# Reads of a DRAM trip moved from the sync engine's queue to ScalarE's, x loaded in 512 B rows, slot numbers read ahead of a wait

## The reference

```
w, sel = top_k(softmax(router_logits), 2); w = w / w.sum(-1)          # per batch
mlp(x, g, u, d) = (gelu(x @ g) * (x @ u)) @ d                         # 256 -> 1024 -> 256
x = x + sum_e dense_w[b, e] * mlp(x, skill_e) + mlp(x, shared)        # layer 0, 8 experts
x = x + x @ w_bot(b).T + bias           # layer 1: w_bot mixed from 8 masked matrices
x = x + base(x) + lora(x) * scaling     # layer 2
x = x + silu(x @ wu[e].T + bu) * (x @ wg[e].T + bg) @ wd[e].T + bd    # layer 3, one expert per batch
```

## Time and profile before

| | |
|---|---|
| time, median of 3 runs | 1145.42 us (1140.33 to 1146.44) |
| the profiled execution | 1153.0 us, span 1151.4 us |
| mean granted TensorE clock | 0.991 |
| TensorE busy | 1118.7 us, 97% of the span |
| DVE, ScalarE, GpSimd busy | 61%, 43%, 40% |
| mean DMA rate | 213 GB/s |

### The profile page before, as it was taken

The page is one execution under the profiler, slowest core; times in us unless marked ns, Lnnn a source line. Parts: engine busy times, 40 slices in busy tenths (PEclk is TensorE's granted clock), DMA queues, the critical chain, the costliest instruction groups (busy, mean ns, idle before and its releaser), DMA issues.

```text
span 1151.4 us, 25095 instructions
## 1 busy us (share of the span) xinstructions
PE 1118.7 (97%) x6894; PEld 958.2 (83%) x6895; DVE 706.8 (61%) x1255; ACT 495.3 (43%) x965; POOL 461.2 (40%) x296
## 2 busy tenths in 40 slices
PE   8999999999899999999998999999999999999998
PEld 6999997788687788878786888889999998878876
DVE  6776676766667576666756676555555555444433
ACT  5356633444343443434333444432222223566664
POOL 3177588405427036180817390100000002887840
PEclk9999999999999999999998999989999999999999
DMA  7269777968779778788788885466644547667753
GB/s 206 75 216 321 281 258 231 278 208 267 208 218 279 225 233 260 239 256 273 225 245 253 249 274 171 140 173 175 165 132 132 136 129 258 205 204 229 234 162 87
DMA packets 257110, 244.94 MB, mean 213 GB/s; under 512 B 89216, under 2 KB 216448, under 8 KB 254976
## 3 DMA queue, kind: packets, MB, share of 16 engines
q1 hardware_dynamic: 217616, 160.39, 47.2%
q0 software_dynamic: 13680, 49.81, 14.6%
q10 hardware_dynamic: 25728, 33.56, 8.2%
HBM read 176.59 MB, written 67.11 MB: 212 GB/s over the span
## 4 chain that ended last, share of the span: by engine, by line
PE 74%; DMA 10%; POOL 5%; DVE 4%; issue 3%; SPq 2%; ACT 1%; POOLq 0%; DVEq 0%; ACTq 0%
PE bank L754 12%; PE bank L755 12%; PE bank L756 12%; PE bank L844 7%; PE bank L1192 6%; PE bank L1221 4%; PE bank L843 3%; DMA squares<-acc 3%; PE bank L1033 2%; PE bank L775 2%; PE bank L1170 2%; DMA FS<-squares 2%; DMA squares<-X 2%; PE bank L895 2%; POOL W L602 2%
## 5 line engine op out<-in xcount | busy, mean ns | idle before, releaser
L600 POOL TENSOR_TENSOR W<-raw,one 128x1024 fp32r<-128x1024 f32 x79 | 150.2, 1901 | 526.6 <-DVE acc L1904 241.3
L754 PE MATMUL bank<-W,RS 128*128 (+1 forms) x512 | 203.5, 397 | 10.3 <-DVE RS L1801 3.2
L1284 ACT ACTIVATE FS<-bank 128x512 f32<-128x512 f32 (+1 forms) x200 | 115.1, 575 | 208.6 <-DVE X L1832 144.9
L755 PE MATMUL bank<-W,RS 128*128 (+1 forms) x512 | 201.2, 393 | 0.0
L756 PE MATMUL bank<-W,RS 128*128 (+1 forms) x512 | 200.8, 392 | 0.0
L602 POOL TENSOR_TENSOR W<-raw,W 128x1024 fp32r<-128x1024 f32 x79 | 191.0, 2417 | 6.2
L844 PE MATMUL bank<-W,RS 128*128 x480 | 172.3, 399 | 4.6 <-DVE RS L1837 4.6
L1837 DVE TENSOR_TENSOR RS<-bank,RS 128x512 fp32r<-128x512 f32 x120 | 82.1, 684 | 96.8 <-ACT RS L1306 96.1
L754 PE MATMUL bank<-RS,W 128*128 128x256 f32 x448 | 130.0, 290 | 1.0 <-DVE RS L1801 1.0
L754 PEld LDWEIGHTS bank<-W,RS 128*128 128x128 f32 x512 | 97.2, 190 | 36.4 <-issue 14.7
L755 PE MATMUL bank<-RS,W 128*128 128x256 f32 x448 | 127.3, 284 | 0.0
(11 more groups left out here) (239 smaller groups left out, 2159.3 us busy)
## 6 DMA issues: line engine op xcount, KB each, us to landing
raw<-in_w POOLq DMA_DIRECT2D x87, 512.0 KB, 5.1
acc<-in_w SPq DMA_DIRECT2D x70, 512.0 KB, 5.5
routing<-squares SPq DMA_DIRECT2D x68, 256.0 KB, 4.0
mixes<-acc SPq DMA_DIRECT2D x16, 1024.0 KB, 6.2
W<-mixes SPq DMA_DIRECT2D x16, 1024.0 KB, 6.2
squares<-X ACTq DMA_DIRECT2D x60, 256.0 KB, 3.3
squares<-acc ACTq DMA_DIRECT2D x60, 256.0 KB, 4.7
FS<-squares SPq DMA_DIRECT2D x52, 256.0 KB, 4.1
```

What stands on the lines that cost most here:

```text
L600: pool.tensor_tensor(hi, raw[:, k, :], ones_like(PIECE), ALU.mult).then_inc(done, 1)
L754: pe.matmul(ps, ah, bh, start=(i == 0), stop=False)
L755: pe.matmul(ps, ah, bl, start=False, stop=False)
L1284: act.activation(gl[h][:, 0:n], gate_ps[h][:, 0:n], ACT.Gelu_apprx_tanh).then_inc(gelu_done, 1)
```

## The change

`read_hidT` moves from the sync engine's program into ScalarE's: the read of the group before for half 1 stands after the second gelu, the read of this group for half 0 after the second write. `load_x` writes whole rows of 512 B into the tile, which now holds batch first; the two consumers (the copy on ScalarE and the subtraction on DVE) view it by depth. At the end of the chosen groups the first `load_chosen` reads its slot numbers ahead of its waits, and stands ahead of the biases instead of behind them; since SP has no reads left, it waits there for the last writes of the squares itself (chosen_in shares memory with a square).

```diff
-                    dst = xraw[p].rearrange("p (c j s) -> p c j s", c=DC, j=2)[:, :, j, :]
-                    sp.dma_start(dst, xT[bass.ds(b, 1)].rearrange("a p c s -> p (a c) s")).then_inc(xraw_in[p], 16)
+                    sp.dma_start(xraw[p][:, P * j:P * (j + 1)], xT[bass.ds(b, 1)].rearrange("a p c s -> p (a c s)"))\
+                        .then_inc(xraw_in[p], 16)
...
-            def load_chosen(n, u, buffer, after=None):
+            def load_chosen(n, u, buffer, after=None, last=()):
                 slots = [s for i in range(4)
                          for s in table_values(sp, slots_of[0:1, bass.ds(8 * u + 2 * i, 2)], SLOTS0 - 1)]
                 if after is not None:
                     sp.wait_ge(x1_done, after)
+                for r, at in enumerate(last):
+                    sp.wait_ge(stored[r], 16 * at.stored)
+                    sp.wait_ge(square_out[r], 16 * NR0)
...
                     load_skill(S0 + s + 2, p, place_at(m, k + 2))
-                    read_hidT(s - 1, 1 - p, 1, before)
...
-                    read_hidT(s, p, 0, at)
...
             load_late(1)
+            load_chosen(0, 0, 0, last=LAST_TWO)
+            store_chosen(S1 - 2, 0, LAST_TWO[0])
             for dst, src in ((b12, b1), (b2s, b2)):
...
-            for r in range(2):
-                sp.wait_ge(stored[r], 16 * LAST_TWO[r].stored)
-            load_chosen(0, 0, 0)
-            store_chosen(S1 - 2, 0, LAST_TWO[0])
...
-                act.activation(xh[xset][p], xraw[p], ACT.Copy).then_inc(xh_done, 1)
+                act.activation(by_depth(xh[xset][p]), raw_by_depth(p), ACT.Copy).then_inc(xh_done, 1)
...
+            def read_hidT(s, p, h, at):
+                n = P if at.half is None else S
+                act.wait_ge(square_out[h], 16 * s + 16)
+                act.dma_start(hidT[p][h].rearrange("p (a x) -> p a x", a=4)[:, :, 0:n],
+                             squares[p, h].rearrange("(a i) (g x) -> (i g) a x", a=4, g=4)[:, :, 0:n])\
+                    .then_inc(hidT_in[p][h], 16)
...
                 gelu(1, 2 * g + 1, n=n, squares=None if isinstance(s, int) and s == 0 else 2 * s)
                 if before_at is not None:
+                    read_hidT(s - 1, 1 - p, 1, before_at)
                     hidden_hi_chosen(s - 1, 1 - p, 0, before_at)
                 write_square(s, p, 1, at)
+                read_hidT(s, p, 0, at)
                 if before_at is not None:
                     hidden_hi_chosen(s - 1, 1 - p, 1, before_at)
```

More of the change, by code:

```diff
@@ L294, in table_values, with by_depth, raw_by_depth @@
                 skip_runtime_bounds_check_because="the routing bounds what the table holds")[1]
+        def by_depth(t):
+            return t.rearrange("p (c j s) -> p c j s", c=DC, j=2)
+        def raw_by_depth(p):
+            return xraw[p].rearrange("p (j c s) -> p c j s", c=DC, j=2)
         def by_chunk(t):
@@ L417, in _ @@
             spill(WPIECES - 1)
[L418 to L424, removed]
             for k in range(NSTAGE):
@@ L428, in _ @@
             load_skill(S0 + 2, 0, place_at(0, 0))
-            read_hidT(0, 0, 0, FIRST_TWO[0])
             load_skill(S0 + 3, 1, place_at(0, 1))
-            read_hidT(0, 0, 1, FIRST_TWO[0])
-            read_hidT(1, 1, 0, FIRST_TWO[1])
             with sp.Fori(0, NMIXED0) as m:
@@ L459, in _ @@
             load_late(0, (0,))
-            read_hidT(NR0 - 3, 1, 1, place(NR0 - 3))
-            read_hidT(NR0 - 2, 0, 0, LAST_TWO[0])
             load_late(0, (1,))
             store_chosen(S1 - 4, 0, place(NR0 - 4))
-            read_hidT(NR0 - 2, 0, 1, LAST_TWO[0])
-            read_hidT(NR0 - 1, 1, 0, LAST_TWO[1])
-            read_hidT(NR0 - 1, 1, 1, LAST_TWO[1])
             store_chosen(S1 - 3, 1, place(NR0 - 3))
             load_late(1)
+            load_chosen(0, 0, 0, last=LAST_TWO)
+            store_chosen(S1 - 2, 0, LAST_TWO[0])
             for dst, src in ((b12, b1), (b2s, b2)):
@@ L1273, in split_x @@
                 if mixed:
-                    act.activation(xm[:, 0:P], xraw[p][:, 0:P], ACT.Copy).then_inc(xh_done, 1)
+                    act.activation(xm[:, 0:P].rearrange("p (j s) -> p j s", j=2), raw_by_depth(p)[:, 0], ACT.Copy).then_inc(xh_done, 1)
                     return
-                act.activation(xh[xset][p], xraw[p], ACT.Copy).then_inc(xh_done, 1)
+                act.activation(by_depth(xh[xset][p]), raw_by_depth(p), ACT.Copy).then_inc(xh_done, 1)
             def gelu(h, n2, first=False, n=512, squares=None):
@@ L1454, in _ @@
             gelu_late(0, 0, squares=2 * NR0 - 1)
+            read_hidT(NR0 - 1, 1, 1, LAST_TWO[1])
             hidden_hi_chosen(NR0 - 1, 1, 0, LAST_TWO[1])
@@ L1798, in split_x @@
                 if mixed:
-                    dve.tensor_copy(xm[:, P:D], xraw[p][:, P:D]).then_inc(xl_done, 1)
+                    dve.tensor_copy(xm[:, P:D].rearrange("p (j s) -> p j s", j=2), raw_by_depth(p)[:, 1]).then_inc(xl_done, 1)
                     return
-                TT(xl[xset][p], xraw[p], xh[xset][p].bitcast(F32), ALU.subtract).then_inc(xl_done, 1)
+                TT(by_depth(xl[xset][p]), raw_by_depth(p), by_depth(xh[xset][p].bitcast(F32)), ALU.subtract).then_inc(xl_done, 1)
             def hidden(h, n2, turned=None, lows=None):
```

## The result

The changed kernel is slower: 1169.34 us, median of 4 runs (1166.64 to 1171.0), against 1143.26 us of the kernel before (4 runs, 1140.33 to 1146.44). The ratio is 1.0195 with a 95% interval of 1.0162 to 1.0227. The profiled execution took 1169.13 us with a span of 1167.5 us.

What follows compares the result with a forecast made beforehand. TensorE was taken as the bound, busy 556.6 of 568 us in the chosen groups. Terms -5.0 - 2.7 + 2.0 - 0.5 - 0.2 = -6.4 took the 1145.4 us median to 1139.0 us; range 1128 to 1158.

Steps and rivals of the forecast that it cites:

- the rival in which ScalarE's loop becomes the bound: Chosen groups: half 1's read lands late and holds up ScalarE, then TensorE; about 1159 us at T = 4.7; chance 0.28.
- Reads leave SP, -7.7: Chosen groups: earlier reads remove one long stall and its low clock, -5.0 us, and smaller stalls, -2.7 us.
- the worst case: One late read of half 1 behind x on SP: stall costs 6.0 us; on ScalarE it would go 2.4 us earlier.
- ScalarE's loop, +2.0: Chosen groups: a loop of 8.0 us has 0.25 us to spare, so single long reads overshoot: +2.0 us.
- T + 3.9: ScalarE's time per group: landing T of half 1's read plus 3.85 us and a wake-up; TensorE needs 8.25 us.
- T = 4.1: Landing time of half 1's read on ScalarE's queue, taken as the median of today's reads, range 2.2 to 9.0 us.
- The wait of half 0, taken as hidden at 7.2 to 7.6 us: ScalarE's read of half 0 waits for its write: write landing 3.3, then 3.9 and a DMA issue inside; no cost.
- The issues, taken at nothing: 136 reads issued on ScalarE, 61 us of its queue at 0.45 each, hidden by gelus or copies; uncovered, 8.9 us.
- x in 512 B rows, -0.5: Loads of x in 128 fewer pieces each, on DMA engines busy 80%: -0.5 us for the whole run.
- the bound of 2.9: Upper limit for the gain from x in 512 B rows: TensorE's 2.9 us of waits for the split of x.
- The handoff, -0.2: End of chosen groups: rows land 2.0 us earlier, but DVE's second add waits for GpSimd's split on the shared port: -0.2 us.

Runs made afterwards that it cites:

- swap: reads_sp with half 1's read of the group before moved ahead of the two loads of x on SP's queue: 1137.92 us, ratio 0.9912 to the kernel before.
- hold_w: reads_sp with half 1's read held on SP until the next square of half 0 is turned, which also releases half 0's write: 1141.9 us.
- xrows: The kernel before with only x in 512 B rows; reads on SP and the old end of the chosen groups stay: 1141.51 us.
- reads_sp: The changed kernel with both halves' reads back on SP; x in 512 B rows and the new order at the end stay: 1142.38 us.
- after: The changed kernel itself, 1169.34 us; the five from it to pair all issue half 1's reads and the squares' writes on ScalarE.
- pair: The changed kernel with both reads of the group before behind ScalarE's split of x, and half 1's write ahead of all copies: 1160.43 us.
- wait_only: reads_sp plus one ScalarE wait for half 0's write to land, where half 0's read had stood, with no DMA: 1150.21 us.
- early: The changed kernel with ScalarE's read of half 1 ahead of the write of half 0 instead of behind the second gelu: 1168.77 us.
- h1_sp: The changed kernel with only half 1's reads back on SP at their old place; half 0's stay on ScalarE: 1168.09 us.
- issue_only: reads_sp plus two small DMAs per group on ScalarE, where the reads had stood, with nothing to wait for: 1149.7 us.
- writes_sp: The changed kernel with the squares' writes issued by SP; ScalarE keeps every wait and both reads: 1149.4 us.
- h0_sp: The changed kernel with only half 0's reads back on SP at their old place; half 1's stay on ScalarE: 1187.73 us.

## Why the prediction was wrong

The forecast of 1139 us was wrong; the rival in which ScalarE's loop becomes the bound is what happened, further out than its top of 1159 us.

*Reads leave SP, -7.7: not borne out.* SP's waits for squares went, and half 1's reads went out 0.56 us behind the write of half 0, 0.5 as put. But they were not earlier: they stood ready 2.66 us on the mean, where SP had kept them 1.07. The prediction followed the worst case and took its gain for the usual one. What could be had there shows with the reads left on SP: swap, which takes x from ahead of half 1's read, is 0.9% under before, some 10 us, though x in 512 B rows has most of that.

*ScalarE's loop, +2.0: the step that failed.* The prediction had a loop of T + 3.9 with T = 4.1, and 8.25 us for TensorE's group. T was 4.35. Around it stood 0.56 + 3.54 = 4.1 us, not 3.9. The 8.25 us are right for a group of two batches (swap starts three in a row at 316.86, 325.11 and 333.36), but the mean of the 64 groups, 8 halves of mixed pairs among them, is 8.05 to 8.09 where nothing holds them up (swap, hold_w, xrows, reads_sp), and a mean landing is to be held against that. The loop is 8.45 against 8.05, so it decides from a mean T of 3.95 on, not from 4.35. Priced as the prediction does, excess times groups, that is 0.4 x 64 = 26 us; the stage lost 25.7. The three means add up to the group's time in any kernel, so this sum says where the time stands and not why. That the loop decides is shown by the runs: the loss goes with the reads (reads_sp), and in 53 of 64 groups ScalarE went straight on from that landing.

*T = 4.1, the term inside it.* The prediction weighed the write ahead on the queue and the weight pieces beside the read against fewer loads of x, and kept today's landing. The pieces were what counted: 4.68 us with one and 4.17 without in the changed kernel, 4.79 and 3.97 over the five kernels from after to pair, and no such difference with the read on SP's queue. The piece's price was there before as well, on half 0's read, which stands behind it on SP's queue (5.28 us with a piece, 3.93 without) and was not in a loop of ScalarE's. This is read off the traces; no run takes the pieces away. The prediction had this cost of leaving SP's queue in its slow rival, but as no term of its sum. In the Trainium skill the page DMA: Bandwidth & Descriptors, section Queues, rings and completion order, says that a DMA engine takes turns between the queues it has work for. The runs agree, 4.79 us beside a piece on the other queue against 3.97 without.

*The wait of half 0, taken as hidden at 7.2 to 7.6 us: also wrong.* By itself it costs 9.0 us in the stage (wait_only), since landings vary and only the long ones count (writes of half 0 there: mean 3.96, the longest 7.1 us); and where half 1's loop is taken away it becomes the bound (early, h1_sp), and its landings, too, are long where SP loads a piece (writes of 256 KB in h1_sp: 4.95 us with, 3.45 without). That is why undoing half of the change gave nothing back.

*The issues, taken at nothing:* 6.4 us for two per group (issue_only).

How the 25.7 us divide stays open. writes_sp gives back 18, but it takes two issues off ScalarE (6.4 by issue_only) and sends the pieces later as well, and loops that run side by side don't add up.

*x in 512 B rows, -0.5: right in sign, too small.* 0.6% or 6.7 us (0.37 to 0.81%), more than the bound of 2.9, which came from a wait that x itself ends; the gain is in what stands behind x on SP's queue.

*The handoff, -0.2: the mechanism was right.* TensorE's wait at the first matmul fell by 0.39 us, but it is 3.90 us in xrows too, which keeps the old order, so the new order can't be given the gain; DVE's second add ends with GpSimd's split either way. The Trainium skill's lock (SBUF — State Buffer, section Who interferes with whom) agrees: that add takes 2.71 us here, 0.69 with GpSimd idle.

## What to carry to other kernels

A DMA that waits should not stand in the program of an engine whose own results are awaited: everything behind it waits too, and read, consumer and next read close a loop whose length is a sum of landings. Weigh such a loop against the undisturbed pace over many groups, not against one pair of starts, with half 1's and half 0's landings apart and for their spread, not their median; and look for the second loop, which takes over when the first is opened. A wait for a landing belongs on an engine with nothing else to do, and before a read changes queues, look at what it had behind it on the old one: on SP's queue the 512 KB piece went after the read, from ScalarE's it is in flight beside it. Here the best place is SP with the read ahead of the loads of x, 0.9% under the kernel before.

## What was not expected of the hardware

- The same 256 KB read takes 4.79 us (mean of five kernels) where SP loads a 512 KB piece from its own queue meanwhile, 3.97 where it loads none; with the piece behind it on one queue it takes 4.04. A 256 KB write ahead of it on its own queue shows no price (4.17 and 3.75 us in after and h0_sp, 4.00 without the write, all without a piece).
- Two DMAs of 8 KB per group on ScalarE, with nothing to wait for, cost 6.4 us in 68 groups, four 12.9; by its own rows one keeps the queue for about 0.5 us (median).
- Loads of x in 128 pieces instead of 256 keep SP's queue 0.88 us a pair instead of 1.31.
